# A transformer block with adaptive layer norm: five sets of conditioning rows instead of eight, the loads moved with them, and four down steps held back to the end

## What is computed

```python
mod = (_silu(L0_c) @ L0_wmod).reshape(L0_c.shape[0], 6, 1, -1)
sa, ca, ga, sb, cb, gb = (mod[:, 0], mod[:, 1], mod[:, 2], mod[:, 3], mod[:, 4], mod[:, 5])
ga = (2 * (ga >= 0) - 1) * jnp.maximum(jnp.abs(ga), 0.25)
gb = (2 * (gb >= 0) - 1) * jnp.maximum(jnp.abs(gb), 0.25)
h = _layernorm(x, axis=-1) * (1 + ca) + sa
x = x + ga * _L0_attn_ref(h, L0_attn_weight, L0_attn_mask)
h = _layernorm(x, axis=-1) * (1 + cb) + sb
x = x + gb * _L0_ffn_ref(h, L0_ffn_Wg, L0_ffn_Wu, L0_ffn_Wd, L0_ffn_ag, L0_ffn_au, L0_ffn_ad)
```

## Time and profile before

| | |
|---|---|
| time, median of 3 runs | 183.68 us (183.35 to 183.94) |
| the profiled execution, its own time | 183.99 us |
| its span, first to last instruction | 182.2 us |
| granted TensorE clock, mean | 0.998 |
| PE busy | 174.1 us, 96% |
| DVE busy | 92.2 us, 51% |
| ACT busy | 83.1 us, 46% |
| POOL busy | 32.4 us, 18% |

### The profile page before, as it was taken

One profiled execution on the slowest core, in us unless ns is written; L12 is line 12 of the kernel. 1 busy time (PEld: TensorE's weight loads), 2 busy tenths in 40 slices (PEclk: granted clock), 3 DMA queues, 4 the chain that ended last, 5 costly groups with the idle time before them and its releaser, 6 DMA issues.

```text
span 182.2 us, 2557 instructions
## 1 busy us (share of the span) xinstructions
PE 174.1 (96%) x920; PEld 132.1 (73%) x920; DVE 92.2 (51%) x191; ACT 83.1 (46%) x118; POOL 32.4 (18%) x42
## 2 busy tenths in 40 slices
PE   6979999999999999999999999999999999999990
PEld 6955546554568778788888888888888888888860
DVE  4853472674493995313544464318644223444274
ACT  3022214838889849724335643464344434342200
POOL 1442330490049220000000000004600000000050
PEclk9999999999999999999999999999999999999999
DMA  5999999998038300000000000000500000000005
GB/s 172 361 410 393 421 413 399 411 403 312 4 86 297 100 4 0 0 4 0 4 0 4 4 2 0 4 4 0 222 12 0 4 0 4 2 4 0 4 17 214
DMA packets 9205, 21.35 MB, mean 117 GB/s; under 512 B 2433, under 2 KB 2433, under 8 KB 8673
## 3 DMA queue, kind: packets, MB, share of 16 engines
q1 hardware_dynamic: 8352, 20.52, 29.7%
q10 hardware_dynamic: 832, 0.54, 0.9%
HBM read 18.96 MB, written 2.10 MB: 116 GB/s over the span
## 4 chain that ended last, share of the span: by engine, by line
PE 90%; DVE 4%; DMA 2%; issue 1%; SPq 1%; DVEq 0%
PE bank L727 44%; PE bank L781 21%; PE bank L697 16%; PE bank L681 3%; PE bank L640 3%; DMA xt<-in_x 2%; PE bank L705 1%; DVE xn L453 1%; DVE xn L564 1%; SPq L207 1%; DVE msum L458 1%; PE bank L653 1%; DVE xt L628 0%; DVE bns L440 0%; PE bank L665 0%
## 5 line engine op out<-in xcount | busy, mean ns | idle before, releaser
L727 PE MATMUL bank<-ht,whi_gu 128*128 128x512 f32 x352 | 84.7, 393 | 0.2 <-issue 0.2
L727 PEld LDWEIGHTS bank<-ht,whi_gu 128*128 128x128 f32 x352 | 65.5, 188 | 14.6 <-issue 1.0
L545 DVE SCALAR_TENSOR_TENSOR awork<-bank,scal,awork 128x512 f32<-128x512 f32 x22 | 16.5, 751 | 54.6 <-PE bank L727 51.7
L781 PE MATMUL bank<-whi_dn,in_split 128*128 128x512 f32 x176 | 43.3, 390 | 0.0
L781 PEld LDWEIGHTS bank<-whi_dn,in_split 128*128 128x128 f32 x176 | 32.9, 188 | 7.0 <-DVE in_split L554 0.2
L697 PE MATMUL bank<-awork,wffn 128*128 128x512 f32 x64 | 31.3, 604 | 0.0
L402 ACT ACTIVATE awork<-bank,scal 128x512 f32<-128x512 f32 x22 | 15.1, 688 | 32.4 <-PE bank L727 31.9
L363 ACT ACTIVATE whi_gu<-wffn 128x1024 fp32r<-128x1024 f32 x22 | 23.2, 1055 | 6.7 <-PE bank L727 6.7
L297 POOL TENSOR_TENSOR xt<-xt,xn 128x512 f32<-128x512 f32 x6 | 7.8, 1320 | 103.9 <-DVE xn L564 103.9
L554 DVE TENSOR_TENSOR in_split<-awork,in_split 128x512 fp32r<-128x512 f32 x22 | 16.2, 737 | 0.8
L356 ACT ACTIVATE junk<-wffn 128x1536 uint8<-128x1536 uint16 x11 | 16.3, 1479 | 0.5
(11 more groups left out here) (50 smaller groups left out, 91.8 us busy)
## 6 DMA issues: line engine op xcount, KB each, us to landing
wffn<-in_w_gu SPq DMA_DIRECT2D x10, 512.0 KB, 11.9
wffn<-in_w_down SPq DMA_DIRECT2D x10, 256.0 KB, 13.3
xt<-in_x SPq DMA_DIRECT2D x8, 256.0 KB, 6.7
modw<-in_mod_ln SPq DMA_DIRECT2D x4, 512.0 KB, 7.0
modw<-in_mod_gate SPq DMA_DIRECT2D x2, 1024.0 KB, 13.0
modw<-in_mod_ln SPq DMA_DIRECT2D x2, 1024.0 KB, 11.3
out<-xt SPq DMA_DIRECT2D x6, 256.0 KB, 2.0
maskt<-in_att_mask SPq DMA_DIRECT2D x4, 256.0 KB, 6.2
```

The costliest lines, as they stand in the source:

```text
L545: dve.scalar_tensor_tensor(inner[:, s % 2, :], bank[gu_bank(s, 1)][:, :], scal[:, c, 1:2], silu_g[:, s % 2, :], ALU.mult, ALU.mult).then_i ...
L727: return pe.matmul(bank[gu_bank(s, u)][:, :], w, h, start=(k == 0 and part == 0), stop=(k == KT - 1 and part == 1))
L781: last = pe.matmul(bank[4 + t][:, :], h, w, start=(c == 0 and part == 0), stop=(c == C - 1 and part == 1))
```

## The change

It does three things. The gate rows of layer 1 are computed in one set with the fourth quarter of the first norm (six blocks), and all rows of the second norm and the second gate in one set of twelve blocks among batch 1's products; that leaves five sets. The fourth set and its column transpose stand later in TensorE's order, the gate transposes earlier by one product. The gate rows are loaded ahead of the x tiles of batch 1, and the second gate's rows right behind the last rows of the second norm. On ScalarE the copy of the set of twelve is followed by four checks. At the end four down steps are held (`HELD`) and done tile by tile; the last step's operands take the place of activations that are no longer read, and VectorE adds all four tiles of batch 1, which ScalarE's queue sends.

```diff
...
 WARM_UP = 18
-BY_POOL = 6
+BY_POOL = TT
 H1_CHUNK = C + -NB * KT * SEQ // (3 * D)
 LAG = 2
+HELD = 4
 SHIFT = BLK + NB
+SETS = KT + 1
+BLOCKS = [2, 2, 2, 2 + KT, 3 * KT]
+MOST = max(BLOCKS)
...
         def whi_d(s):
-            return whi_dn[:, s % 3, :]
+            return ht[:, 0, 1, 0, :] if s == STEPS - 1 else whi_dn[:, s % 3, :]
+        def inner_part(s, part):
+            return ht[:, 0, 0, part, :] if s == STEPS - 1 else in_split[:, s % 3, part, :]
...
                 load_att(k)
+            sp.dma_start(modw[:, 2, :, :], mod_gate[0]).then_inc(d_gate[0], 16)
             for t in range(TT, NB * TT):
                 load_x(t)
-            sp.dma_start(modw[:, 2, :, :], mod_gate[0]).then_inc(d_gate[0], 16)
             sp.wait_ge(rows_done, 2)
...
                     sp.dma_start(modw[:, 1, :, :], mod_ln2[1]).then_inc(d_ln2[1], 16)
+                    sp.dma_start(modw[:, 2, :, :], mod_gate[1]).then_inc(d_gate[1], 16)
                 if c < C - 1:
...
                       .then_inc(d_ffn[c], 16)
-                if c == 4:
-                    sp.wait_ge(rows_done, KT + 1)
-                    sp.dma_start(modw[:, 2, :, :], mod_gate[1]).then_inc(d_gate[1], 16)
             for n in range(BY_POOL):
...
             act.activation(sc[:, :, :].rearrange("p j (i m) -> p j i m", m=SHIFT)[:, :, :, 0:NB],
-                           condt[:, :, :].unsqueeze(2).to_broadcast([P, KT, KT, NB]), ACT.Silu)\
+                           condt[:, :, :].unsqueeze(2).to_broadcast([P, KT, MOST, NB]), ACT.Silu)\
                .then_inc(silu_c, 1)
-            ROWS_BANK = [6, 6, 6, 6, 6, 2, 2, 3]
-            ROWS_SLOT = [0, 1, 0, 1, 2, 0, 1, 2]
-            ROWS_LAST = {2: 0, 3: 1, 5: 2, 6: 3, 7: 4}
...
                 act.wait_ge(rows_done, n + 1)
-                if n in ROWS_LAST:
-                    act.wait_ge(cols_done, ROWS_LAST[n] + 1)
-                act.activation(rows[:, ROWS_SLOT[n], :], bank[ROWS_BANK[n]][:, 0:P], ACT.Copy)\
+                if n >= 2:
+                    act.wait_ge(cols_done, n - 1)
+                act.activation(rows[:, n % 2, :], bank[6 if n < KT else 2][:, 0:P], ACT.Copy)\
                    .then_inc(rows_copied, 1)
...
             def round_d(s):
-                if s >= 3:
+                if s == STEPS - 1:
+                    act.wait_ge(up_mm, C)
+                elif s >= 3:
                     wait_down(act, s - 3)
...
             check_chunk(next(check_at))
-            copy_rows(5)
-            check_chunk(next(check_at))
-            copy_rows(6)
-            for _ in range(3):
+            copy_rows(KT)
+            for _ in range(4):
                 check_chunk(next(check_at))
...
-            def sum_columns(use, count, src):
-                dve.wait_ge(cols_done, use + 1)
-                part = src[:, 0:P].rearrange("p (j r) -> p r j", r=BLK)[:, 0:count * NB, :]
-                dve.tensor_reduce(colv[:, use, 0:count, :].rearrange("p i b -> p (i b)"), part, AX_X, ALU.add)\
-                   .then_inc(cols_ok, 1)
-                dve.wait_ge(cols_ok, use + 1)
             def mod_columns(n):
-                use = n if n < KT else n + 1
-                count = 2 if n < KT else KT
-                sum_columns(use, count, bank[7 if n < KT else 7 - n])
+                dve.wait_ge(cols_done, n + 1)
+                part = bank[7 if n < KT else 3][:, 0:P].rearrange("p (j r) -> p r j", r=BLK)
+                dve.tensor_reduce(colv[:, n, 0:BLOCKS[n], :].rearrange("p i b -> p (i b)"),
+                                  part[:, 0:BLOCKS[n] * NB, :], AX_X, ALU.add).then_inc(cols_ok, 1)
+                dve.wait_ge(cols_ok, n + 1)
                 dve.wait_ge(consts_ok, 6)
-                dst = modc[:, 0, n, :] if n < KT else \
-                    modc[:, 1, 2 * (n - KT):2 * (n - KT) + 2, :].rearrange("p k v -> p (k v)")
-                dve.tensor_tensor(dst, colv[:, use, 0:count, :].rearrange("p i b -> p (i b)"),
+                count = 2 if n < KT else 2 * KT
+                dst = modc[:, 0, n, :] if n < KT else modc[:, 1, :, :].rearrange("p k v -> p (k v)")
+                dve.tensor_tensor(dst, colv[:, n, 0:count, :].rearrange("p i b -> p (i b)"),
                                   oneplus[:, 0:count * NB], ALU.add).then_inc(modc_ok, 1)
...
-            def guard_gate(layer, src):
-                use = KT if layer == 0 else 2 * KT - 1
-                sum_columns(use, KT, src)
-                g = colv[:, use, :, :]
+            def guard_gate(layer):
+                use, first = (KT - 1, 2) if layer == 0 else (KT, 2 * KT)
+                dve.wait_ge(cols_ok, use + 1)
+                g = colv[:, use, first:first + KT, :]
                 half_sign, gate = gscr[:, layer, :, :], gcol[:, layer, :, :]
...
                 dve.wait_ge(inner_ok, s + 1)
-                if s >= 3:
+                if 3 <= s < STEPS - 1:
                     wait_down(dve, s - 3)
-                hi, lo = in_split[:, s % 3, 0, :], in_split[:, s % 3, 1, :]
+                hi, lo = inner_part(s, 0), inner_part(s, 1)
                 dve.tensor_copy(hi, inner[:, s % 2, :]).then_inc(in_hi, 1)
...
         def _(pe):
-            def mod_rows(n, count, src, dst):
-                if n == 0:
-                    pe.wait_ge(silu_c, 1)
-                for i in range(count):
-                    for j in range(KT):
-                        last = pe.matmul(dst[BLK * j:BLK * (j + 1), 0:P], sc[:, j, i * BLK:(i + 1) * BLK],
-                                         src(j)[:, i * P:(i + 1) * P], start=(i == 0), stop=(i == count - 1))
+            def mod_rows(n, parts, dst):
+                at = 0
+                for count, src in parts:
+                    for i in range(count):
+                        for j in range(KT):
+                            last = pe.matmul(dst[BLK * j:BLK * (j + 1), 0:P],
+                                             sc[:, j, at * BLK:(at + 1) * BLK],
+                                             src(j)[:, i * P:(i + 1) * P],
+                                             start=(at == 0), stop=(at == BLOCKS[n] - 1))
+                        at += 1
                 last.then_inc(rows_done, 1)
...
                     pe.wait_ge(rows_copied, k)
+                else:
+                    pe.wait_ge(silu_c, 1)
                 m = modw[:, k // 2, 2 * (k % 2):2 * (k % 2) + 2, :].rearrange("p a n -> p (a n)")
-                mod_rows(k, 2, lambda j: m[:, j * (D // 2):(j + 1) * (D // 2)], bank[6])
+                parts = [(2, lambda j: m[:, j * (D // 2):(j + 1) * (D // 2)])]
+                if k == KT - 1:
+                    pe.wait_ge(d_gate[0], 16)
+                    parts.append((KT, lambda j: modw[:, 2, j, :]))
+                mod_rows(k, parts, bank[6])
+            def rows_later():
+                pe.wait_ge(d_ln2[0], 16)
+                pe.wait_ge(d_ln2[1], 16)
+                pe.wait_ge(d_gate[1], 16)
+                pe.wait_ge(att_read, 3)
+                mod_rows(KT, [(KT, lambda j: modw[:, 0, j, :]), (KT, lambda j: modw[:, 1, j, :]),
+                              (KT, lambda j: modw[:, 2, j, :])], bank[2])
...
                 for part in range(2):
-                    h = in_split[:, s % 3, part, t * P:(t + 1) * P]
+                    h = inner_part(s, part)[:, t * P:(t + 1) * P]
                     w = whi_d(s)
...
-                o, a, z = STEPS - 3, STEPS - 2, STEPS - 1
+                o, p, a, z = range(STEPS - HELD, STEPS)
                 pe.wait_ge(in_lo, a + 1)
...
                 def products(native):
-                    for i, (s, t) in enumerate([(o, 0), (a, 0), (o, 1), (a, 1), (o, 2), (z, 0),
-                                                (z, 1), (a, 2), (z, 2), (o, 3), (a, 3), (z, 3)]):
-                        if i == 5:
-                            pe.wait_ge(in_lo, z + 1)
-                            pe.wait_ge(wd_hi, z + 1)
-                        down_product(s, t, native)
+                    for s in (o, p, a):
+                        down_product(s, 0, native)
+                    for s in (o, p):
+                        down_product(s, 1, native)
+                    pe.wait_ge(in_lo, z + 1)
+                    pe.wait_ge(wd_hi, z + 1)
+                    down_product(z, 0, native)
+                    for s in (a, z):
+                        down_product(s, 1, native)
+                    for t in (2, 3):
+                        for s in (o, p, a, z):
+                            down_product(s, t, native)
...
-            def gate_rows():
-                pe.wait_ge(d_gate[0], 16)
-                pe.wait_ge(rows_copied, KT)
-                mod_rows(4, KT, lambda j: modw[:, 2, j, :], bank[6])
-            def gate_columns():
-                pe.wait_ge(rows_copied, KT + 1)
-                pe.wait_ge(modc_ok, KT)
-                columns(2, bank[7])
             def gate_first(b):
                 pe.wait_ge(gate_m, 1)
+                pe.wait_ge(rows_copied, KT)
```

(63 more changed lines are left out.)

## The result

The changed kernel took 187.58 us (median of 4 runs, 186.05 to 188.38) beside 183.81 for the kernel before: 1.7% slower, ratio 1.0171 with an interval of 1.0105 to 1.0237. Two later series gave 186.06 (6 runs, ratio 1.0105, 1.0063 to 1.0146) and 186.74 (12 runs, ratio 1.0100, 1.0065 to 1.0135). The ratios leave out runs more than about 1.5% above the fastest of their kernel; the medians hold all. I had forecast 184.3 and a range up to 185.4. Slower it was, but by 2 to 4 us instead of 0.6.

A forecast was written before the change was run, and what follows sets the result against it. TensorE bounds the kernel, 90% of the span, at full clock. Shift at gate_up(2) +2.98, FFN -1.34, end -1.04: +0.60 us, so 184.3 against the median (184.6 for an execution like the profiled one); range 183.4 to 185.4.

The forecast's parts named there:

- the one on the clock: TensorE behind the new stop: the array stays as fast as before, so no time is added for a lower clock.
- The sum: Whole kernel: 2.98 - 1.34 - 1.04 = +0.60 us, at full clock.
- fourth rival: The clock falls behind the stop, up to 3.0 us and at least half: 185.8 to 187.3; chance 0.07.
- The first stop: TensorE stands 2.04 us ahead of transposes(4), waiting for xn; with 0.15 for an unhidden load, transposes(4) start 1.86 later.
- The sets: TensorE's sets cost 0.22 us a block plus 0.13 each: 1.45 for six blocks, 2.77 for twelve.
- ScalarE's chain: Four checks behind the long set's copy make ScalarE 2.98 us late, holding TensorE at transposes(10) (0.3) and gate_up(2).
- The shift at gate_up(2): gate_up(2) waits for ScalarE's rounding and starts 2.98 us later than before, at 62.8.
- gate_up_first: Its start, behind the wait at transposes(10), comes at 55.0, 2.7 us later than before.
- The FFN: Layer 1's gate set and column transpose leave TensorE's queue there, and no wait replaces them: -1.34 us.
- The end: The last gate starts at once after the last product, instead of behind a slow VectorE add: -1.04 us.
- third rival: The end gives nothing or little, through a slow add or longer transfers: +0.65 to +1.04, 184.9 to 185.3; chance 0.10.
- The loads: Loads that change places, and the three times longer memset of sc in VectorE's opening, cost nothing.

The follow-up runs named there:

- a5_busy_stop: Changed kernel with eight identity products on TensorE in the stop ahead of transposes(4); 185.38 us, ratio 1.0055 to the kernel before.
- a6_open_busy: Changed kernel with the opening's pauses filled by extra products (two more warm-up products too), stop left empty; 186.76 us.
- a9_changed_again: The changed kernel, unchanged, run again to count its low-clock runs beside the kernel before; 186.74 us.
- a3_checks_first: Changed kernel with three ScalarE checks ahead of the long set's copy and two behind, instead of one and four; 186.36 us.
- a0_again: The changed kernel, unchanged, run again; 186.06 us, six runs from 184.67 to 187.97.
- a7_all_busy: Changed kernel with products filling both the opening's pauses and the stop ahead of transposes(4); 185.02 us, ratio 1.0043 to the kernel before.
- a4_both: Changed kernel with stats(1,2) and stats(1,3) ahead of mod_columns(3), and three checks ahead of the long set's copy; 182.50 us, ratio 0.9903.
- b4_long_stop: Kernel before with ten memsets on VectorE in normalise(1), so TensorE stands about 10 us ahead of transposes(4); 196.37 us.
- a1_stats_first: Changed kernel with stats(1,2) and stats(1,3) ahead of mod_columns(3) on VectorE; 182.74 us, ratio 0.9916 to the kernel before.
- b2_tail_new: Kernel before with only the changed kernel's end: four down steps held, batch 1's adds on VectorE, sent from ScalarE's queue; 183.08 us, ratio 0.9941.

## Why the prediction was wrong

**The step that failed** is the one on the clock: "The sum takes the array as fast behind the new stop, since the pause of 0.79 us ahead of 10.28, its longest, was followed by matmuls at the later pace." The sum put the clock at nothing. A pause of 0.79 us in one execution says nothing of one of 2.07, and not even of itself: in 17 of 90 runs the kernel before loses clock, and the low profile of a5_busy_stop puts its loss behind just this opening. I had the mechanism as fourth rival, with a chance of 0.07 and a price of 1.5 to 3.0. It was the rule: 16 of 22 runs were low, at 1.6 to 1.7 us for the fall behind the stop. The place is shown by the windows of a6_open_busy and a9_changed_again, the cause by the fillings: five of six low with the stop empty, none of twelve with it filled as well. What decides whether a given execution keeps its clock over the stop (6 of 22 did) is open.

The runs at 0.982 or less took 187.9 to 188.5 us, some 3 more than at full clock. I took this for both falls in one run. That is not shown: no profile holds such a run, and the kernel before, which has no stop, reaches 0.982 and 186.8 to 187.8 us in nine of its 90 runs.

The Trainium skill (TensorE: Matmul & The Clock Gate, the part on the clock gate) has the array fall back to 1.2 GHz when it idles; the rows agree, the granted clock goes to 0.50 and a linear from 0.86 to 1.54.

**What held.** By its own steps, for an execution at full clock:
- The first stop: forecast 2.04 us, measured 2.07; the transposes behind it took 0.66 instead of 0.44, so 0.22 where I took 0.15.
- The sets: 1.45 us for six blocks, as forecast, 2.80 for twelve (2.77).
- ScalarE's chain: a3_checks_first takes it away and gains 0.5 to 0.7. The shift at gate_up(2) was 64.26 - 1.31 - 59.82 = 3.13, forecast 2.98; it was 56.63 - 1.31 - 52.35 = 2.97 at gate_up_first (forecast 2.7), so more of it arose ahead of that place, and less at the pause, than I had it.
- The FFN: the shift falls from 3.13 to 180.32 - 1.31 - 177.2 = 1.8: -1.3, as forecast.
- The end: -1.04 forecast, -1.05 measured alone. My third rival falls.
- The loads cost nothing; VectorE took up the first x tile at 3.51 in spite of the longer memset of sc, at 3.55 before.

By full-clock runs, each against the kernel before in the same series, the changed kernel is 1.0 us slower in a0_again and 0.8 in a9_changed_again; with the stop filled, which takes the same time, it is 0.8 (a5_busy_stop) and 1.0 (a7_all_busy). The profiles give 0.7 to 0.9 behind the opening. So the sum of 0.6 was 0.2 to 0.4 short; 0.15 of that is the shift at gate_up(2), the rest is not placed.

**Where the gain went.** Sets and end together are worth 2.0 to 2.1 us: the seven runs of a4_both at full clock have a median of 182.0, the kernel before 184.0 in the same series, and behind the first column transpose the profiles have 169.8 and 171.9. The fourth set, moved behind two linears and four transposes and made longer, held VectorE's queue at mod_columns(3) with two unrelated statistics behind it; that cost 2.3 us as a stop and 1.7 more as lost clock in most executions. Exchanging the three lines gives both back.

## What to carry to other kernels

An operation that is moved later on one engine holds up everything that stands behind its reader in the other engine's queue; put work that doesn't need it ahead of the wait. Where TensorE would stand for 2 us, count the fall of its clock too: 1.7 us here, in most executions. If the wait can't be removed, a few products of the identity into a free bank kept the clock here (none of twelve runs low instead of five of six), and they cost nothing: transposes(4) started 20.1 us behind the first column transpose with them and without.

Look at the granted clock of every run, not of the one that was profiled: here two profiles of the slow kernel showed no fall at all.

## What the runs showed of the hardware

- A stop of 2.07 us was followed by a granted clock of 0.50 from about 31.6 until 35.0 (a6_open_busy). It comes 0.7 us behind the stop's end at 30.93, when TensorE is at work again, so all of it lies on useful products. In a9_changed_again it comes at the stop's end: the windows from 30 to 36 read 0.72, 0.50 and 0.93, and transposes(4) took 1.12 us. In the stop of 10.34 us of b4_long_stop it came inside the stop.
- The opening's pauses of 0.73, 0.79 and 0.55 us within 4.3 us, one after the other, were followed by a fall as well in the profile of a5_busy_stop, and pauses of 1.39, 0.79 and 0.55 us were not in that of a1_stats_first. With the last two filled and no stop left none of 18 runs was low; in the series of a7_all_busy the kernel before had seven of 23 beside its none of twelve. That the low runs of the kernel before all come from its opening is inferred, no profile of it shows one.
- The granted clock read 1.00 over the first 7 us, while 36 records of 128 columns took 0.19 us each (in other profiles 5.8 us and more for the 36), so its full reading there is no proof of a fast array. Behind a fall the reading and the records agree: 0.50 and twice the time.
- One run of b2_tail_new, its profiled one, read a steady 0.95 from 5 us to the end of its products and took 183.90 us, 0.8 above the median; nothing here explains it. One of the kernel before took 255.94 at 0.663.
